# The first 33 score units of an attention and mixture-of-experts block take queries and keys as projected

## The chip, the cores and the metric

The kernel runs on one core of a Trainium2 chip. The metric is the time of one execution on the device in microseconds, the median of several runs. The core's engines are called PE (matrix products), DVE (vector), ACT (scalar functions), POOL (general purpose) and SP (here it only issues DMAs). They run their own instruction streams and meet at semaphores.

## What is computed

Four batch elements of 512 tokens with 256 features go through one transformer block. The first half, with 16 heads of 16 features, is:

```python
h = _layernorm(x, axis=-1) * (1 + ca) + sa
qkv = jnp.einsum('bsh,oh->bso', x, Wqkv) + bqkv
scores = jnp.einsum('bhqd,bhkd->bhqk', q, k) * scale
scores = jnp.where(causal, -jnp.inf, scores)
attn = jax.nn.softmax(scores, axis=-1)
out = jnp.einsum('bhqk,bhkd->bhqd', attn, v)
x = x + ga * _L0_attn_ref(h, ...)
```

The second half normalises again, sends each token to the best of 8 experts, adds a shared expert, and adds the gated sum to x. The gates and shifts (`sa, ca, ga, sb, cb, gb`) come from a small product with `wmod`.

## The kernel before

Products keep float32 accuracy by halves: an operand is split into a float16 high part and a float16 remainder ("low"), and one product is made as high·high, high·low and low·high.

The attention of a batch element b is a loop of 44 steps (`BU`), n = 0 to 43, in each engine's stream. A step holds one **score unit** N of up to 512 columns. The scores are computed twice. The first time, `scores(N)` on PE gives queries on the partitions, and `maxima(N)` on DVE takes each query's maximum. The second time, `scores_t(N)` gives keys on the partitions with the negated maximum built in, and ACT exponentiates the result (`exps`, line 846). The first kind runs ahead of the second by `LAG` = 33 units. So there is a head, b = -1, whose steps n = 11 to 43 hold units 0 to 32 of element 0 and nothing of the second kind. Eleven units make a group of four heads: one of 4 × 128 columns, two of 2 × 256, four of 384 and four of 512.

The units read **stacks**: `qs` and `ks` hold for each head 126 rows with high, high, low of the queries against high, low, high of the keys, so that one product of 126 rows makes all three. Stacks are built through memory. PE projects (`project_qk`, four parts u of an element: queries and keys, each in two halves f), ACT adds the bias and writes high parts and float32 (`qk_parts`, line 835), POOL subtracts for the low parts (`qk_low`, line 700). Then SP stores six pieces to `qk_d` (`qk_out`, line 462) and, when they have landed, loads four back (`stacks`, line 479). Maxima take the same way: DVE negates them (`negate`, lines 1074 and 1075), SP stores them (`maxima_out`, line 489) and loads them into the stacks (line 496).

Meanwhile the experts' weights are split in the background in 27 pieces k. SP loads piece k into `stage` (`stage_load`, lines 512 and 514), ACT makes the high half (`split_high`, line 896), DVE the low half (`split_low`, line 1167), and SP stores both to `w_d` (`halves_out`, line 518). The table `SPLITS` says after which step each split stands: pieces 0 and 1 in the head at steps 18 and 26, pieces 2, 3 and 4 at steps 4, 9 and 14 of element 0. There are two buffers for halves, so the high half of piece 2 waits until `halves_out(0)` has landed, and that of piece 4 until `halves_out(2)` has:

```python
if 2 <= k < BOUNCED:
    ac.wait_ge(s_bw[k % 2], 16 * (k // 2))
```

Other work (projections of the next elements, normalisation, output) stands at steps by the table `SIDE`. These jobs share a bank on PE (`M1`): each waits until the job before it has left it. SP's stream is written out by hand, and every DMA on it waits for the one ahead to be issued. Small rows `mod_d` (line 547) carry the gates through memory.

## Time and profile before

| | us |
|---|---|
| median of 3 runs | 474.42 |
| lowest and highest run | 473.86, 476.61 |
| profiled execution, whole | 479.8 |
| its span | 478.1 |
| PE busy in it | 402.4 |
| DVE busy in it | 310.0 |
| ACT busy in it | 226.8 |

The profiled execution is one of its own; its rows give durations and places in microseconds from the start of the span. "Idle before" is how long the engine had waited, and the arrow names what ended the wait. The head lasts until about 69 us; the rest of element 0 follows until about 124 us.

### The profile page before, as it was taken

How to read it: one execution, taken by the hardware profiler on the slowest of the kernel's cores; microseconds unless marked ns; L12 is line 12 of the kernel's file. 1: busy time of each engine (PE TensorE's matmuls, PEld its weight loads, DVE VectorE, ACT ScalarE, POOL GpSimd, SP SyncE). 2: the span in 40 equal slices, each digit the busy share in tenths (PEclk: the TensorE clock that was granted, in tenths of full speed). 3: DMA queues.
4: the chain of work that ended last, by engine and by line, in shares of the span. 5: the costliest groups of instructions: out<-in, count | busy, mean ns of one | idle time of the engine just before them, and what ended most of it. 6: DMA issues, size and time to landing. Idle time of an engine off the chain costs nothing.

```text
span 478.1 us, 8357 instructions
## 1 busy us (share of the span) xinstructions
PE 402.4 (84%) x2898; PEld 227.9 (48%) x2898; DVE 310.0 (65%) x629; ACT 226.8 (47%) x403; POOL 209.0 (44%) x251
## 2 busy tenths in 40 slices
PE   3767677889978789988879968999968999999991
PEld 3233233444544345444434434565645666666661
DVE  3823697876898968999977753789734444444441
ACT  2533424867666666755677636345122232323220
POOL 1457393374226763358331762110600555555332
PEclk9997789999999999998999989999989999999998
DMA  8568548765678557652433001994621344434210
GB/s 258 170 154 212 147 117 259 265 196 136 168 264 293 156 127 167 222 179 88 169 81 99 2 0 52 354 360 161 180 86 44 65 80 85 78 74 81 32 21 0
DMA packets 45921, 67.95 MB, mean 142 GB/s; under 512 B 5365, under 2 KB 33653, under 8 KB 45881
## 3 DMA queue, kind: packets, MB, share of 16 engines
q1 hardware_dynamic: 40200, 58.76, 40.6%
q0 software_dynamic: 5152, 8.14, 8.6%
q8 instruction: 25, 0.41, 0.4%
q10 hardware_dynamic: 528, 0.52, 0.3%
q14 instruction: 16, 0.12, 0.1%
HBM read 43.14 MB, written 25.18 MB: 143 GB/s over the span
## 4 chain that ended last, share of the span: by engine, by line
PE 51%; DVE 17%; DMA 8%; POOL 7%; issue 7%; ACT 6%; SPq 3%; ACTq 0%; DVEq 0%; POOLq 0%
PE bank L1411 35%; DVE mx L1066 5%; PE bank L1525 4%; PE bank L1509 3%; DVE rowg L1167 2%; PE bank L1739 2%; PE bank L1481 2%; DMA qk_d<-W 2%; POOL W L719 2%; DMA w_d<-rowg 2%; DMA mod_d<-h2T 1%; ACT rowg L896 1%; DMA stage<-in_gup 1%; POOL rowg L727 1%; POOL rowg L726 1%
## 5 line engine op out<-in xcount | busy, mean ns | idle before, releaser
L846 ACT ACTIVATE W<-bank 128x512 f32<-128x512 f32 (+1 forms) x176 | 94.8, 564 | 65.1 <-PE bank L1509 63.3
L1066 DVE TENSOR_REDUCE mx<-bank 128x1 f32<-128x384 f32 (+3 forms) x176 | 104.8, 632 | 20.2 <-PE bank L1483 19.9
L1411 PE MATMUL bank<-W 128*128 128x256 f16 (+2 forms) x756 | 106.5, 293 | 10.2 <-POOL W L694 3.4
L1411 PEld LDWEIGHTS bank<-W 128*128 128x128 f16 x756 | 73.3, 100 | 44.3 <-issue 14.2
L1481 PE MATMUL bank<-W 126*128 126x128 f16 (+3 forms) x256 | 67.0, 318 | 20.6 <-DVE mx L1066 17.2
L719 POOL TENSOR_SCALAR_AFFINE_SELECT W<-W 128x512 f32<-128x512 f32 x64 | 45.3, 713 | 79.7 <-ACT W L846 79.7
L1411 PE MATMUL bank<-W,h2T 128*128 x276 | 68.4, 385 | 4.9 <-DVE W L1182 4.0
L1509 PE MATMUL bank<-W 128*128 128x512 f16 (+3 forms) x256 | 63.1, 304 | 5.2 <-ACT W L846 3.5
L789 POOL DMA_INDIRECT out<-h2T,sidx x23 | 36.3, 1578 | 69.5 <-DVE h2T L1381 69.2
L1525 PE MATMUL bank<-W 128*32 128x128 f32 (+3 forms) x512 | 48.4, 451 | 8.7 <-POOL W L719 8.7
L1483 PE MATMUL bank<-maskb,identb 128*128 128x128 bf16 (+2 forms) x176 | 45.3, 257 | 0.0
L1411 PE MATMUL bank<-h2T,W 128*128 128x512 f16 x192 | 43.1, 379 | 0.6 <-DVE W L1182 0.6
L1481 PEld LDWEIGHTS bank<-W 126*128 126x128 f16 x256 | 24.0, 102 | 40.3 <-DVE mx L1066 28.7
L1411 PEld LDWEIGHTS bank<-W,h2T 128*128 128x128 f16 x276 | 27.1, 98 | 30.8 <-issue 10.6
L1509 PEld LDWEIGHTS bank<-W 128*128 128x128 f16 x256 | 21.5, 98 | 40.3 <-ACT W L846 18.5
L1374 DVE TENSOR_TENSOR W<-bank,W 128x512 f16<-128x512 f32 x23 | 15.9, 692 | 37.4 <-ACT W L979 37.4
L979 ACT ACTIVATE W<-bank 128x512 f16<-128x512 f32 x23 | 13.8, 598 | 55.0 <-PE bank L1739 47.9
L775 POOL DMA_INDIRECT rowg<-h_d,gidx x23 | 23.2, 1009 | 31.4 <-DVE gidx L1324 24.7
L1167 DVE SCALAR_TENSOR_TENSOR rowg<-stage,rowg 128x1024 f16<-128x1024 f32 x18 | 25.2, 1398 | 17.7 <-ACT rowg L896 17.7
L835 ACT ACTIVATE W<-bank,bqk 128x512 f16<-128x512 f32 (+1 forms) x32 | 20.3, 687 | 24.2 <-PE bank L1411 24.2
L1411 PEld LDWEIGHTS bank<-h2T,W 128*128 128x128 f16 x192 | 18.5, 98 | 21.9 <-DVE W L1182 1.0
L700 POOL TENSOR_TENSOR W<-W 128x512 f16<-128x512 f32 x16 | 18.5, 1157 | 17.0 <-ACT W L835 16.7
(163 smaller groups left out, 522.7 us busy)
## 6 DMA issues: line engine op xcount, KB each, us to landing
w_d<-rowg SPq DMA_DIRECT2D x18, 512.0 KB, 3.9
W<-w_d SPq DMA_DIRECT2D x18, 512.0 KB, 8.0
stage<-in_gup SPq DMA_DIRECT2D x16, 512.0 KB
qk_d<-W SPq DMA_DIRECT2D x48, 128.0 KB
W<-qk_d SPq DMA_DIRECT2D x32, 192.0 KB, 4.4
stage<-in_down SPq DMA_DIRECT2D x8, 512.0 KB
x_sb<-in_x SPq DMA_DIRECT2D x4, 512.0 KB, 8.9
h_d<-gbb SPq DMA_DIRECT2D x4, 512.0 KB, 4.5
```

Of the source, the lines that this page charges most:

```text
L719: g.affine_select(out=d, in_=d, compare_op=ALU.is_ge, fill=0.0, base=0, pattern=[[0, 4], [1, P]], channel_multiplier=-1).then_inc(s_msk, 1)
L775: g.indirect_dma_start(rowg[:, r % RG, :], None, h2_d, bass.IndirectOffsetOnAxis(ap=gidx[:, r:r + 1].bitcast(U32), axis=0)).then_inc(s_gr[ ...
L789: g.indirect_dma_start(out.rearrange("b s n -> (b s) n"), bass.IndirectOffsetOnAxis(ap=sidx[:, r:r + 1].bitcast(U32), axis=0), ry[r % YR], ...
L835: a.activation(dst, side_bank("qk", b, u)[:, :], ACT.Identity, bias=bqk[:, 2 * isk + u // 2:2 * isk + u // 2 + 1], scale=1.0 / WS if isk e ...
L846: a.activation(PT[j][:, i:i + m, :], t_bank(N)[:, 0:m * w].rearrange("p (i n) -> p i n", i=m), ACT.Exp).then_inc(s_exp, 1)
L1066: v.tensor_reduce(mx_v[:, b % 2, hp0 // 4, par, i:i + m, t], SB[N % 3][:, 0:m * w].rearrange("p (i n) -> p i n", i=m), AX.X, ALU.max).then ...
L1167: v.scalar_tensor_tensor(split_part(k, 1), staged(k), WS, split_part(k, 0), ALU.mult, ALU.subtract).then_inc(s_el, 1)
L1411: i = t_.matmul(outp, l, r, start=(n == 0), stop=(n == len(prods) - 1), **kw)
L1481: t_.matmul(bk[:, w * i:w * (i + 1)], qs[r][0:P - 2, hp, par, P * t:w], ks[r][0:P - 2, hp, 0:w], start=(i == 0), stop=False, skip_group_ch ...
L1483: t_.matmul(bk[:, 0:m * w].rearrange("p (i n) -> p i n", i=m)[:, :, w - P:w], identb[:, :], maskb[:, :].unsqueeze(1).to_broadcast([P, m, P ...
L1509: q = t_.matmul(t_bank(N)[:, w * i:w * (i + 1)], ks[r][:, hp, P * j:P * (j + 1)], qs[r][:, hp, par, P * j:S], start=True, stop=True)
L1525: q = t_.matmul(OTb[32 * i:32 * i + 32, P * j:S], v1[b % 2][:, c:c + 32], PT[j][:, i], start=(j == 0), stop=(j == TT - 1), tile_position=( ...
```

## The change

Units 0 to 32 no longer read the stacks. `scores_apart` reads the projected queries and keys (`qk0`, now apart from the `qk16` of the other elements) where they lie: 32 partitions hold two neighbouring heads of 16 rows. A copy `qz` of the queries has the other head's rows multiplied by zero (`query_parity` on DVE, eight operations, with a column from `parity_columns`). Each head then takes three products of 32 rows where one of 126 rows stood, and a mask of its own. Neighbouring units go in pairs on two banks and on different 32 rows of the array. Units with several heads run head after head, with a wait (`s_tile`) between them. The head's units rotate over four banks.

The head's table is new (`HEAD`): the jobs for element 1 stand later, the projections at steps 26, 28, 31 and 33, and the splits 0 and 1 at steps 24 and 36. SP's stream is changed in one place. The stacks are still built, for `scores_t` and for the units from 33 on.

```diff
-SPLITS = {-1: {18: 0, 26: 1},
+SPLITS = {-1: {24: 0, 36: 1},
+HEAD = [(12, "stats1", 1, 0), (16, "v", 0, 0), (17, "norm1", 1, 0), (18, "v", 0, 1), (20, "turn", 1, 0),
+        (22, "turn", 1, 1), (26, "qk", 1, 0), (28, "qk", 1, 1), (31, "qk", 1, 2), (33, "qk", 1, 3),
+        (34, "max", 0, 0)]
...
             qk_out(1, 0)
+            maxima_out(0, 0)
+            maxima(0, 0)
             stacks(1, 0)
             qk_out(1, 1)
-            maxima_out(0, 0)
-            maxima(0, 0)
             stacks(1, 1)
...
+            def scores_apart(pair):
...
+                for i in range(m):
+                    c = slice(w * i, w * (i + 1))
+                    if i:
+                        pe.wait_ge(s_tile, n_tile[0])
+                    for N in pair:
+                        t_.matmul(s_bank(N)[:, w * (i + 1) - P:w * (i + 1)], identb[:, :], maskb[:, :],
+                                  start=(i == 0), stop=False, skip_group_check=True)
+                    for p, (cq, ck) in enumerate(((0, 0), (0, 1), (1, 0))):
+                        for N in pair:
+                            j = 32 * (QU[N % UNITS][1] + i)
+                            q = t_.matmul(s_bank(N)[:, c], qz[j:j + 32, cq, f, par, P * t:w],
+                                          qk0[j:j + 32, 2 + ck, f, 0:w], start=False,
+                                          stop=(p == 2 and i == m - 1), skip_group_check=True)
...
+            def query_parity(f, c):
+
+                ve.wait_ge(*((s_ql, 2 * f + 1) if c else (s_qh, 2 * f + 1)))
+                for par in range(2):
+                    v.tensor_scalar(qz[:, c, f, par], qk0[:, c, f], pick[:, par:par + 1], None,
+                                    ALU.mult).then_inc(s_qz, 1)
```

**SP, behind the three loads of `stage` in the head.** `W<-qk_d` are stacks, `ng_d` the maxima, `w_d<-rowg` a store of halves. Before:

```order
L479 DMA W<-qk_d 48x4x512 [waits s_zero,s_const,s_qkw1_0]
L479 DMA W<-qk_d 48x4x512 x3
L462 DMA qk_d<-W 8x16x512 [waits s_qh]
L462 DMA qk_d<-W 8x16x512 x3
L462 DMA qk_d<-W 8x16x512 [waits s_ql]
L462 DMA qk_d<-W 8x16x512
L489 DMA ng_d<-negm 32x2x128 [waits s_neg]
L496 DMA W<-ng_d 2x4x512 [waits s_ngw]
L496 DMA W<-ng_d 2x4x512
L479 DMA W<-qk_d 48x4x512 [waits s_qkw1_1]
L479 DMA W<-qk_d 48x4x512 x3
L518 DMA w_d<-rowg 128x2048 [waits s_el]
```

And after:

```order
L515 DMA ng_d<-negm 32x2x128 [waits s_neg]
L522 DMA W<-ng_d 2x4x512 [waits s_ngw]
L522 DMA W<-ng_d 2x4x512
L505 DMA W<-qk_d 48x4x512 [waits s_zero,s_const,s_qkw1_0]
L505 DMA W<-qk_d 48x4x512 x3
L488 DMA qk_d<-W 8x16x512 [waits s_qh]
L488 DMA qk_d<-W 8x16x512 x3
L488 DMA qk_d<-W 8x16x512 [waits s_ql]
L488 DMA qk_d<-W 8x16x512
L505 DMA W<-qk_d 48x4x512 [waits s_qkw1_1]
L505 DMA W<-qk_d 48x4x512 x3
L544 DMA w_d<-rowg 128x2048 [waits s_el]
```

The store and load of the maxima now stand ahead of the first stacks and of the second set of six stores of element 1, where they stood behind both.

**ACT, between the second job `turn` of element 1 and its projections.** Lines 835 and 861 are `qk_parts`, lines 896 and 922 the split of piece 0. Before:

```order
L835 ACTIVATE W<-bank7,bqk 128x512 [waits s_h1l,s_qkw0_0,s_qkv]
L835 ACTIVATE W<-bank7,bqk 128x512
L896 ACTIVATE rowg<-stage 128x1024 [waits s_eld0]
L835 ACTIVATE W<-bank7,bqk 128x512 [waits s_h1l,s_qkv]
L835 ACTIVATE W<-bank7,bqk 128x512
```

And after:

```order
L922 ACTIVATE rowg<-stage 128x1024 [waits s_eld0]
L861 ACTIVATE W<-bank7,bqk 128x512 [waits s_h1l,s_qkv]
L861 ACTIVATE W<-bank7,bqk 128x512
L861 ACTIVATE W<-bank7,bqk 128x512 [waits s_h1l,s_qkv]
L861 ACTIVATE W<-bank7,bqk 128x512
```

The first of the four parts of element 1 stood ahead of the split; now all four stand behind it.

**PE, in front of the transposition of the maxima** (lines 1489 and 1571). Lines 1481 and 1563 are products of 126 rows, 1483 and 1536 masks, 1541 products of 32 rows, 1411 and 1463 projections. Before, the last units ahead of it are of 512, 4 × 128 and 2 × 256 columns:

```order
L1481 MATMUL bank<-W 128x512
L1483 MATMUL bank<-maskb,identb 128x128
L1481 MATMUL bank<-W 128x128 x4
L1483 MATMUL bank<-maskb,identb 128x512
L1481 MATMUL bank<-W 128x256 x2
L1483 MATMUL bank<-maskb,identb 128x2x128
L1489 MATMUL bank<-ident,mx 32x128
```

And after:

```order
L1463 MATMUL bank<-W 128x512 x6
L1536 MATMUL bank<-maskb,identb 128x128 x2
L1541 MATMUL bank<-W 128x256 x6
L1536 MATMUL bank<-maskb,identb 128x128 x2
L1541 MATMUL bank<-W 128x256 x6
L1571 MATMUL bank<-ident,mx 32x128
```

The fourth projection of element 1, which stood eight steps earlier, now stands right ahead of units 23 and 24 (12 products of 256 columns), and these ahead of the transposition.

## Rows read from the trace of the kernel before

**Rows 1.** The timeline of SP: start, duration, line, what is issued, how many.

```profile
28.41 1.81 SPq L479 DMA_DIRECT2D W<-qk_d  x4
30.27 3.68 SPq L462 DMA_DIRECT2D qk_d<-W  x6
38.61 1.77 SPq L479 DMA_DIRECT2D W<-qk_d  x4
40.43 0.94 SPq L512 DMA_DIRECT2D stage<-in_gup  x2
...
48.54 3.65 SPq L462 DMA_DIRECT2D qk_d<-W  x6
55.07 1.79 SPq L479 DMA_DIRECT2D W<-qk_d  x4
...
65.71 0.31 SPq L489 DMA_DIRECT2D ng_d<-negm  x1
...
67.70 1.76 SPq L479 DMA_DIRECT2D W<-qk_d  x4
69.50 0.44 SPq L518 DMA_DIRECT2D w_d<-rowg  x1
```

**Rows 2.** The timeline of ACT: start, duration, instruction, idle before it and its end.

```profile
46.88 1.06 ACT L896 ACTIVATE rowg<-stage 128x1024 f16<-128x1024 f32 x1 [3.88 <-DMA stage<-in_gup]
47.84 1.25 ACT L835 ACTIVATE W<-bank,bqk 128x512 f16<-128x512 f32 x2
...
69.55 2.77 ACT L846 ACTIVATE W<-bank 128x512 f32<-128x512 f32 x5 [9.08 <-PE bank L1509]
75.64 1.06 ACT L896 ACTIVATE rowg<-stage 128x1024 f16<-128x1024 f32 x1 [3.32 <-DMA w_d<-rowg]
...
87.64 1.06 ACT L896 ACTIVATE rowg<-stage 128x1024 f16<-128x1024 f32 x1 [1.01 <-DMA w_d<-rowg]
```

**Rows 3.** The timeline of DVE and PE where ACT stands at piece 2.

```profile
76.73 1.23 DVE L1167 SCALAR_TENSOR_TENSOR rowg<-stage,rowg 128x1024 f16<-128x1024 f32 x1 [2.46 <-ACT rowg L896]
...
77.14 0.34 PE L1509 MATMUL bank<-W 128*128 128x384 f16 x1 [1.32 <-ACT W L846]
```

**Rows 4.** The chain that ended last, two of its longest pieces behind the head.

```profile
72.24 7.14 DMA mod_d<-h2T
80.25 7.31 DMA w_d<-rowg
```

**Rows 5.** The timeline of PE in the head.

```profile
16.41 7.10 PE L1411 MATMUL bank<-W 128*128 128x512 f16 x24 [3.35 <-POOL W L694]
...
26.97 1.48 PE L1411 MATMUL bank<-W 128*128 128x256 f16 x12
...
35.16 0.61 PE L1481 MATMUL bank<-W 126*128 126x128 f16 x4 [2.84 <-DMA W<-qk_d]
...
43.05 1.47 PE L1411 MATMUL bank<-W 128*128 128x512 f16 x6 [0.81 <-ACT W L835]
...
51.32 2.77 PE L1411 MATMUL bank<-W 128*128 128x512 f16 x6
```

**Rows 6.** Busy time by stretch: PE, PEld, DVE, ACT, POOL, then clock, DMA, GB/s.

```profile
49.80:53.80 4.00, 3.95 (x14) 1.91 (x15) 3.10 (x6) 0.00 (x0) 0.52 (x1) 0.50 0.52 167
```

**Rows 7.** Groups by shape, 16 to 79 us: count, busy, mean ns, idle before.

```profile
L1066 DVE TENSOR_REDUCE mx<-bank 128x1 f32<-128x512 f32 x10 | 6.3, 678 | 1.1 <-PE bank L1483 1.1
L1066 DVE TENSOR_REDUCE mx<-bank 128x1 f32<-128x384 f32 x12 | 6.0, 544 | 1.5 <-PE bank L1483 1.5
...
L1053 DVE SCALAR_TENSOR_TENSOR W<-h2T,W 128x512 f16<-128x512 f32 x1 | 0.7, 681 | 0.0
...
L1483 PE MATMUL bank<-maskb,identb 128*128 128x128 bf16 x30 | 7.3, 242 | 0.0
```

**Rows 8.** The timeline of DVE and PE: negation, and products on single groups of columns.

```profile
65.10 0.27 DVE L1074 TENSOR_SCALAR negm<-bank 32x128 f16<-32x128 f32 x1
...
65.41 0.28 DVE L1075 SCALAR_TENSOR_TENSOR negm<-bank,negm 32x128 f16<-32x128 f32 x1
...
23.44 3.60 PE L1427 MATMUL bank<-stage,cs 128*4 128x512 f32 x8
...
78.86 1.06 PE L1525 MATMUL bank<-W 128*32 128x512 f32 x8
```

More of the change, by code:

```diff
@@ L96 @@
 FIRST = [(2, 4, 7), (7, 10, 13), (13, 15, 18)]
+HEAD = [(12, "stats1", 1, 0), (16, "v", 0, 0), (17, "norm1", 1, 0), (18, "v", 0, 1), (20, "turn", 1, 0),
+        (22, "turn", 1, 1), (26, "qk", 1, 0), (28, "qk", 1, 1), (31, "qk", 1, 2), (33, "qk", 1, 3),
+        (34, "max", 0, 0)]
 def side_jobs(b, n):
-    early = 6 if b < 0 else 0
-    jobs = [(job, b + d, part) for at, job, d, part in SIDE
-            if at - (min(early, at - 2) if d == 2 else 0) == n and 0 <= b + d < B]
+    if b < 0:
+        return [(job, c, part) for at, job, c, part in HEAD if at == n]
+    jobs = [(job, b + d, part) for at, job, d, part in SIDE if at == n and 0 <= b + d < B]
     if b == B - 1:
@@ L235, in build @@
         aT = early(2 * KC * S, F16).rearrange("p (s k n) -> p s k n", s=2, k=KC)
+        at[0] = first
+        qk0 = early(4 * 2 * S, F16).rearrange("p (a c n) -> p a c n", a=4, c=2)
+        qz = early(4 * 2 * S, F16).rearrange("p (c f two n) -> p c f two n", c=2, f=2, two=2)
         bc = early(2 * 3 * H).rearrange("p (r n) -> p r n", r=2)
@@ L262, in build, with s_bank, before, qk_halves @@
         SB = [S0, S1, T2]
+        def s_bank(N):
+            return [S0, S1, T2, OTb][N % 4] if N < LAG else [T2, S0, S1][N % 3]
+        def before(N):
+            return max((n + 1 for n in range(max(N - 4, 0), N) if s_bank(n) is s_bank(N)), default=0)
+        def qk_halves(b):
+            return qk16 if b else qk0
         def t_bank(N):
@@ L927, in _ @@
                         exps(BU * b + n)
+                    if b < 0 and n == 15:
+                        modulation_rows()
+                        other_high()
                     if n % UNITS == 4 and G > 0:
@@ L1460, in project_v @@
                 i.then_inc(s_qkv, 1)
+            n_tile = [0]
+            def scores_apart(pair):
+                gr = pair[0] // UNITS
+                par, f = gr % 2, gr // 2
+                t, _, m = QU[pair[0] % UNITS]
+                w = P * (t + 1)
+                if pair[0] == 0:
+                    pe.wait_ge(s_const, 2)
+                    pe.wait_ge(s_col, 1)
+                if pair[0] % (2 * UNITS) == 0:
+                    pe.wait_ge(s_qz, 4 * f + 4)
+                    pe.wait_ge(s_ql, 2 * f + 2)
+                if max(before(N) for N in pair):
+                    pe.wait_ge(s_mx, max(before(N) for N in pair))
+                for i in range(m):
[11 more added lines that the diff above has]
+                                          stop=(p == 2 and i == m - 1), skip_group_check=True)
+                            if p == 2 and i == m - 1:
+                                q.then_inc(s_s1, 1)
+                    if i < m - 1:
+                        n_tile[0] += 1
+                        q.then_inc(s_tile, 1)
             def scores(N):
@@ L1500, in scores_t @@
                     pe.wait_ge(s_mr, 2)
-                before = [n for n in range(max(N - 3, 0), N) if t_bank(n) is t_bank(N)]
-                if before:
-                    pe.wait_ge(s_exp, before[-1] + 1)
+                    pe.wait_ge(s_stk[0][0], 16 * 4)
+                used = [n for n in range(max(N - 3, 0), N) if t_bank(n) is t_bank(N)]
+                if used:
+                    pe.wait_ge(s_exp, used[-1] + 1)
                 if t_bank(N) is T2:
@@ L1517, in values @@
                     pe.wait_ge(s_v, TT * (b + 1))
-                if j == 0 and G:
-                    pe.wait_ge(s_ote, G)
+                if j == 0:
+                    pe.wait_ge(*((s_ote, G) if G else (s_mx, LAG)))
                 pe.wait_ge(s_msk, 4 * G + j + 1)
```

94 lines of the change are left out of this document (58 added, 36 removed).

## The prediction

> **What bounds the kernel now.** I read the waits first. In the head, PE stands until the stacks have landed: the first unit starts at 35.16 us, after 2.84 us of waiting, while the projections ended at 23.51 [rows 5]. The change is aimed at these 11.65 us. But the head's end is not what ACT waits for last. ACT exponentiates the first five units from 69.55 us, and then waits 3.32 us, until 75.64, for the store of halves [rows 2]. DVE stands at the same piece 2 (2.46 us of waiting) and PE behind ACT's banks (1.32 us) [rows 3]. So at 75.64 us all three engines stand at one point. It depends on one DMA, the store that SP issued at 69.50 [rows 1]. Two long pieces of the chain that ended last, 72.24 to 79.38 and 80.25 to 87.56, are the DMAs that SP issued next [rows 4], and ACT waits once more, 1.01 us, until 87.64 [rows 2]. **The question is therefore when SP issues the store of halves 0 (line 518), not when the first unit starts.** Until it has landed, whatever the head gains is waited away.
>
> **SP before.** Negated maxima leave at 65.71, the last stacks at 67.70, the store at 69.50: 3.79 us from negation to store [rows 1].
>
> **SP after.** Behind the negation stand: store and load of the maxima; the stacks (1,0); the six stores of part f = 1 of element 1; their landing; the stacks (1,1); then the store of halves.
> - Store and load of the maxima: 65.71 to 67.70, 1.99 us [rows 1].
> - The rest: the rows have the very sequence once, for element 0: stacks at 28.41, six stores from 30.27, stacks at 38.61, next issue at 40.43. That is 12.02 us. The lower bound takes the landing from the third set, which nothing was in front of: 48.54 to 55.07 is 6.53 us, with stacks of 1.81 ahead and 1.79 behind, 10.13 us [rows 1]. I take 12.02, since here too four stacks go out right ahead of the stores.
> So negation to store is 14.0 us (12.1 to 14.0) against 3.79. To come out even, the negation would have to end 10.2 us earlier than at 65.7, at 55.5.
>
> **When the negation ends after.** Its start is anchored by a load that the change leaves alone: SP's stream up to the loads of `stage` at 40.43 us is the same, so piece 0 lands at 46.88 as before, ACT makes its half and reaches `qk_parts` at 47.84 [rows 1, 2]. Before, this was the second part of element 1. After, it is the first, since all four now stand behind the split. It ends at 49.1. Three projections are left, each behind ACT's reading of the one before it. On PE the following stand in a row, in the new order:
> - projection, part 1: six products of 512 columns, 1.47 us [rows 5]
> - units 18, 19 and units 20, 21: a pair is six products of 512 columns in all, as a projection is, so 1.47 us if they run one after the other and about 0.75 if they run two by two, with 0.1 for masks: 3.1 or 1.7 us for both pairs [rows 5]
> - projection, part 2: 1.47 us
> - unit 22, four heads one after the other, in each a mask and three products of 128 columns; one takes 0.242 us from start to end, and 0.06 more for each that follows in the stream [rows 5, 7]: about 1.7 us
> - projection, part 3: 1.47 us
> - units 23, 24: 12 products of 256 columns, 1.48 us, or half, with masks and one wait between heads 0.4: 1.9 or 1.1 us [rows 5]
> - transposition and negation: from the rows 0.27 and 0.28 us with what lies between, about 1.0 [rows 8]
> ACT's 1.25 us for each part [rows 2] is covered by the pairs, but for 0.2 us once where they run side by side. The sums are 12.1 and 10.1 us, so the negation ends at 61.2 or 59.2 us. The rows show PE's clock at 0.50 from 49.8 to 53.8, after it had stood idle, and a projection at 51.32 taking 2.77 us in place of 1.47 [rows 5, 6]. PE will again wait for ACT before 49 us. A clock at half for one projection adds 1.3 us, for the pair behind it up to 1.5: 63 us at most. I take **60.5 us**, between 59.2 and 63.
>
> DVE does not bound this: from 49.2 us on it has 10 maxima of 0.54 to 0.68 us [rows 7], 6.4 us, against PE's 10 or more.
>
> **What goes before 49 us at no cost.** DVE's eight operations on the queries are not in the trace. The bounds are 0.27 us (negation, 128 columns) and 0.68 (a remainder of 512 columns) [rows 7, 8], so 2.2 to 5.4 us; I take 2.4. PE's first unit starts about 24 us. Fourteen units must be through by 47.9, when DVE will stand at the split, and side jobs of some 7 us lie between; at 0.68 a unit DVE needs 17 of the 22 us. The slack is 3 to 5 us, and it covers the longer operations, the extra products (three of 32 rows for each of 126) and the gates' products, 3.60 us [rows 8]. Without that cover each microsecond would be paid once.
>
> **Two rules of the Trainium skill.** The trace has matmuls side by side only on groups of columns: eight records of 512 columns take 1.06 us, where eight on one place took 3.60 [rows 8]. Of groups of rows no row tells. "TensorE: Matmul & The Clock Gate", in its part on packing small matmuls, says that products on different row groups run together; by it the negation would end at 59.2 and the time would be about 478.1. "TensorEngine Tiling (Array Packing)", Key Properties, says that a change of the tiling mode drains the engine. Masks here take the whole array and the products 32 rows, so each step would be drained twice; by that rule the 61.2 would be nearer. Neither gives another sign.
>
> **The sum.** 60.5 + 14.0 = 74.5 us for the issue of the store, against 69.50: 5.0 us later. Bounds: 59.2 + 12.1 = 71.3, so 1.8 us later; 63 + 14.0 = 77.0, so 7.5 later. As ACT, DVE and PE all wait at that point, and the DMAs next on SP (4) stand behind the same store, nothing absorbs it: ACT waited 3.32 us and will wait longer, since its exponentials start earlier, at about 65.5 us (five maxima and the split of piece 1, 1.23 us, lie between the negation and the bank of the last unit). Behind this point the order of all streams is as before, so the rest moves as a whole. The profiled execution was 479.8 us (span 478.1), 5.4 over the median of 474.42; the shift applies to either. 479.8 becomes 484.8, and the median **479.4 us**.
>
> **Rivals.**
> 1. *The order on SP costs almost nothing.* Products side by side, PE's clock at full and the stores landed as fast as in the third set: 1.8 us later, 476.2; with DVE or ACT a little sooner 1 us, 475.4. For it: PE stays busy longer before 49 us. Against it: two independent favourable cases. Chance 0.18.
> 2. *The head's gain arrives: faster.* The place is ACT's wait at piece 2. If the store of halves were issued ahead of where it was, the gain would be the earlier start of the second kind of units, 69.1 to about 65: 4 us, 470.4. It decides at a negation that ends at 55.5 us. It needs three projections and their reading, 3 × (1.47 + 1.25) from 49.1, to be over at 54.5 already without this rival's units; they are over at 57.3. It is possible only if piece 0 lands well ahead of 46.88. Chance 0.07.
> 3. *The small products are the bound.* At half clock a 512-column product takes 0.43 us (the first of the 24 at 16.41 ran so). If the 32-row products leave PE's clock there, and run one after the other, a unit of 1,583 columns on average takes 1.3 us and some waits, about 1.7 instead of 0.9; over the 16 units until the second projection that is 13 us, less 3 of slack: 10 us more, 489 (and up to 9 more if the low clock stays to the negation). For it: a group of eleven units has 17,408 columns where it had 7,168. Against: PE is busier than before, and idleness went ahead of the low clock in [rows 5, 6]. Chance 0.09.
> 4. *The change does not do what it says*, the units still wait for something near 35 us: then unit 13 is reached at about 52, and the shift is 3 us more than forecast, 482. It is inside my case, not counted apart.
>
> **How the numbers follow.** The forecast case, 2.4 to 9 us later, has 0.66. Left out of the range are rival 2 (0.07), rival 3 (0.09) and little else, so the range goes from 474.9 to 485.5. About 0.5% is what a measurement of this kernel can tell from no change, 2.4 us. Faster by more: rival 2, 0.07. Within: rival 1, 0.18, with some of it beyond, 0.17. Slower by more: 0.76.
>
> **What would show it.** Right: the first unit of 32 rows at about 24 us; ACT's first split still at 46.9; negation at 59 to 63; the store of halves issued at 72 to 77; ACT's wait for `w_d` at piece 2 grown from 3.3 us to about 12, and the split there at about 80.6. Overlap of pairs shows in two products of one pair starting together. Wrong: a negation before 56, a store of halves before 70, or an ACT that is not waiting for it at piece 2. If piece 0 lands several microseconds earlier or later, the anchor is wrong and all moves with it.

## The result and the profile after

The changed kernel took 481.17 us in the median (480.63 to 483.48), the kernel before beside it 475.38 us (473.86 to 476.61): a ratio of 1.0113, with a 95% interval of 1.0076 to 1.0150. It is slower, by 5.8 us. The ratios and intervals in this document are taken over the fast runs alone and need not equal the quotient of the medians, which cover all runs (the two differ by up to 0.3%). The profiled execution took 481.26 us, with a span of 479.5 us and a clock of 0.956.

| | before | after |
|---|---|---|
| first unit on PE | 35.16 us | 23.80 us |
| ACT's split of piece 0 | 46.88 | 47.34 |
| negation ends | 65.69 | 61.10 |
| store of halves 0 issued | 69.50 | 75.53 |
| ACT's split of piece 2 | 75.64 | 81.51 |
| ACT's split of piece 4 | 87.64 | 93.31 |

The timeline of SP after, the answer to [rows 1]: start, duration, line, what is issued, how many.

```profile
61.12 0.34 SPq L515 DMA_DIRECT2D ng_d<-negm  x1
62.60 0.56 SPq L522 DMA_DIRECT2D W<-ng_d  x2
63.27 1.76 SPq L505 DMA_DIRECT2D W<-qk_d  x4
65.08 3.66 SPq L488 DMA_DIRECT2D qk_d<-W  x6
73.71 1.77 SPq L505 DMA_DIRECT2D W<-qk_d  x4
75.53 0.44 SPq L544 DMA_DIRECT2D w_d<-rowg  x1
```

The maxima leave at 61.12, 4.6 us earlier than the 65.71 of [rows 1]. The store of halves leaves at 75.53, 6.0 us later than the 69.50 there. Between them lie 14.41 us in place of 3.79. SP issues nothing from 68.74 (the end of the six stores) to 73.71: it waits until the stores have landed. The chain that ended last has this landing as a piece, and the two pieces of [rows 4] again behind it:

```profile
68.16 5.54 DMA qk_d<-W
...
78.23 6.88 DMA mod_d<-h2T
...
85.98 7.24 DMA w_d<-rowg
```

The timeline of ACT, the answer to [rows 2]. The last columns are the idle time before an instruction and what ended it.

```profile
47.34 1.06 ACT L922 ACTIVATE rowg<-stage 128x1024 f16<-128x1024 f32 x1 [3.03 <-DMA stage<-in_gup]
48.44 1.26 ACT L861 ACTIVATE W<-bank,bqk 128x512 f16<-128x512 f32 x2
...
58.58 1.26 ACT L861 ACTIVATE W<-bank,bqk 128x512 f16<-128x512 f32 x2 [2.14 <-PE bank L1463]
...
67.14 0.60 ACT L872 ACTIVATE W<-bank 128x512 f32<-128x512 f32 x1 [5.05 <-PE bank L1592]
...
81.51 1.06 ACT L922 ACTIVATE rowg<-stage 128x1024 f16<-128x1024 f32 x1 [9.72 <-DMA w_d<-rowg]
```

The first exponential starts 2.4 us earlier than in [rows 2], and the wait for the store of halves has grown from 3.32 to 9.72 us. DVE and PE stand at the same place, as in [rows 3]. The timeline of DVE, then that of PE:

```profile
19.41 0.61 DVE L1261 TENSOR_SCALAR W<-W,pick 128x512 f16<-128x512 f16 x2 [1.92 <-ACT W L861]
...
22.09 6.11 DVE L1261 TENSOR_SCALAR W<-W,pick 128x512 f16<-128x512 f16 x6
...
60.82 0.28 DVE L1106 SCALAR_TENSOR_TENSOR negm<-bank,negm 32x128 f16<-32x128 f32 x1
...
82.60 1.23 DVE L1198 SCALAR_TENSOR_TENSOR rowg<-stage,rowg 128x1024 f16<-128x1024 f32 x1 [8.76 <-ACT rowg L922]
```

```profile
45.68 2.72 PE L1463 MATMUL bank<-W 128*128 128x512 f16 x6 [0.25 <-POOL W L719]
...
49.76 2.15 PE L1463 MATMUL bank<-W 128*128 128x512 f16 x6
51.74 0.28 PE L1536 MATMUL bank<-maskb,identb 128*128 128x128 bf16 x2
51.95 0.82 PE L1541 MATMUL bank<-W 32*128 32x512 f16 x6
52.70 0.28 PE L1536 MATMUL bank<-maskb,identb 128*128 128x128 bf16 x2
...
53.67 1.47 PE L1463 MATMUL bank<-W 128*128 128x512 f16 x6
54.98 0.22 PE L1536 MATMUL bank<-maskb,identb 128*128 128x128 bf16 x1
55.13 0.34 PE L1541 MATMUL bank<-W 32*128 32x128 f16 x3
55.53 0.23 PE L1536 MATMUL bank<-maskb,identb 128*128 128x128 bf16 x1
...
65.10 1.46 PE L1541 MATMUL bank<-W 32*128 32x512 f16 x6
...
83.00 0.50 PE L1592 MATMUL bank<-W 128*128 128x384 f16 x1 [7.62 <-ACT W L872]
```

From 81.51 us on everything is shifted as a whole: the split of piece 4 by 5.67 us, of piece 6 (106.28 against 100.50) by 5.78, and of the last piece, 26 (278.87 against 273.12), by 5.75. The medians differ by 5.79.

The two profiled spans, 478.1 and 479.5 us, differ by less. The busy time by stretch shows why. Its columns are those of [rows 6]. First before, then after:

```profile
330.00:350.00 20.00, 16.71 (x115) 10.02 (x113) 14.48 (x36) 4.70 (x9) 8.33 (x8) 1.00 0.51 159
350.00:370.00 20.00, 17.00 (x107) 11.11 (x108) 8.07 (x17) 4.41 (x9) 0.00 (x0) 0.91 0.08 27
```

```profile
330.00:350.00 20.00, 19.32 (x158) 12.08 (x156) 17.93 (x51) 7.62 (x13) 5.14 (x6) 1.00 0.47 157
350.00:370.00 20.00, 17.31 (x114) 11.01 (x112) 9.74 (x20) 4.79 (x9) 3.67 (x3) 1.00 0.35 110
```

The execution of before that was profiled has 2.6 us more idle PE time in the first stretch and a clock of 0.91 in the second. The first scatter of results on POOL behind them is shifted by only 2.06 us (372.18 and 374.24). So the profiled execution of before lost 3.7 us in between which the other did not. This stretch, from the split of piece 26 to the first scatter, takes 94.7 to 100.4 us over the profiled executions, and not by their head: 99.06 in before, 95.37 in the changed kernel, but 99.4 and 100.4 in e3 and e1, which are changed kernels too. The execution of before was also 5.4 us above its own median. The shift up to piece 26 is therefore the better measure of the change, and the medians agree with it.

### The profile page after: what moved, and what is told of

The parts are those of the page before. It is cut to its first block, busy times and chain, and to the rows that moved or that the text cites. A ratio compares the mean times of both kernels' runs of the same rounds, so it can differ in the third digit from the quotient of the medians.

```text
span 479.5 us, 8593 instructions
## 1 busy us (share of the span) xinstructions
PE 414.1 (86%) x3009; PEld 230.8 (48%) x3009; DVE 317.1 (66%) x639; ACT 226.7 (47%) x403; POOL 210.3 (44%) x251
## 4 chain that ended last, share of the span: by engine, by line
PE 55%; DVE 17%; POOL 7%; issue 6%; ACT 6%; DMA 5%; SPq 2%; ACTq 0%; DVEq 0%; POOLq 0%
PE bank L1463 35%; PE bank L1608 4%; DVE mx L1097 4%; PE bank L1592 3%; PE bank L1829 2%; DVE rowg L1198 2%; PE bank L1563 2%; PE bank L1541 2%; POOL W L745 2%; ACT W L847 2%; DMA w_d<-rowg 2%; DMA mod_d<-h2T 1%; POOL rowg L753 1%; POOL rowg L752 1%; DMA qk_d<-W 1%
## 5 line engine op out<-in xcount | busy, mean ns | idle before, releaser
L1097 DVE TENSOR_REDUCE mx<-bank 128x1 f32<-128x384 f32 (+3 forms) x176 | 105.7, 633 | 19.1 <-PE bank L1565 11.3
L1463 PE MATMUL bank<-W 128*128 128x256 f16 (+2 forms) x756 | 107.9, 295 | 8.2 <-POOL W L719 3.6
L1592 PE MATMUL bank<-W 128*128 128x512 f16 (+3 forms) x256 | 65.1, 312 | 11.5 <-ACT W L872 9.8
L1463 PE MATMUL bank<-W,h2T 128*128 x276 | 67.2, 380 | 1.8 <-DVE W L1213 1.0
L1563 PE MATMUL bank<-W 126*128 126x128 f16 (+3 forms) x208 | 54.7, 314 | 6.5 <-DVE mx L1097 6.5
L1565 PE MATMUL bank<-maskb,identb 128*128 128x128 bf16 (+2 forms) x143 | 36.2, 253 | 0.0
L1563 PEld LDWEIGHTS bank<-W 126*128 126x128 f16 x208 | 19.5, 100 | 18.3 <-DVE mx L1097 11.7
L726 POOL TENSOR_TENSOR W<-W 128x512 f16<-128x512 f32 x16 | 19.7, 1233 | 16.1 <-ACT W L861 15.9
```

The lines of the kernel that those rows point to most:

```text
L1097: v.tensor_reduce(mx_v[:, b % 2, hp0 // 4, par, i:i + m, t], s_bank(N)[:, 0:m * w].rearrange("p (i n) -> p i n", i=m), AX.X, ALU.max).then ...
L1463: i = t_.matmul(outp, l, r, start=(n == 0), stop=(n == len(prods) - 1), **kw)
L1563: t_.matmul(bk[:, w * i:w * (i + 1)], qs[r][0:P - 2, hp, par, P * t:w], ks[r][0:P - 2, hp, 0:w], start=(i == 0), stop=False, skip_group_ch ...
L1565: t_.matmul(bk[:, 0:m * w].rearrange("p (i n) -> p i n", i=m)[:, :, w - P:w], identb[:, :], maskb[:, :].unsqueeze(1).to_broadcast([P, m, P ...
L1592: q = t_.matmul(t_bank(N)[:, w * i:w * (i + 1)], ks[r][:, hp, P * j:P * (j + 1)], qs[r][:, hp, par, P * j:S], start=True, stop=True)
```

## The experiments

There are two theories. **A**: the store of halves stands behind stores, a landing and stacks on SP, and that order alone costs the time. **B**: the new head (products of 32 rows, later projections) costs it. A landmark serves for all runs: the start of ACT's split of piece k, in us.

| kernel | k = 2 | 4 | 6 | 7 | 26 | ratio to before |
|---|---|---|---|---|---|---|
| before | 75.64 | 87.64 | 100.50 | 124.19 | 273.12 | 1 |
| changed | 81.51 | 93.31 | 106.28 | 129.95 | 278.87 | 1.0113 |
| a0_changed_again | 81.06 | 92.80 | 105.83 | 129.50 | 278.51 | 1.0132 |
| e1_sp_order | 79.58 | 91.34 | 104.57 | 128.25 | 278.70 | 1.0077 |
| e2_before_sp | 87.01 | 98.62 | 111.78 | 135.47 | 284.43 | 1.0236 |
| e3_stores_first | 72.15 | 92.92 | 106.22 | 129.89 | 278.86 | 1.0108 |
| e4_split_late | 82.08 | 93.85 | 106.70 | 130.37 | 279.24 | 1.0140 |
| e6_unit_by_unit | 82.39 | 94.17 | 107.16 | 130.84 | 279.81 | 1.0168 |
| e5_stores_free | 74.05 | 85.65 | 105.97 | 129.11 | 279.55 | 1.0082 |
| e7_before_free | 72.65 | 84.40 | 105.49 | 128.63 | 279.08 | 1.0095 |
| e8_maxima_first | 72.33 | 83.94 | 97.85 | 125.12 | 274.02 | 0.9985 |
| e9_before_maxima | 73.91 | 85.68 | 99.61 | 125.06 | 274.10 | 1.0005 |
| e10_maxima_again | 71.69 | 83.29 | 97.22 | 120.91 | 269.85 | 0.9951 |
| e11_before_again | 73.07 | 84.84 | 98.77 | 122.44 | 271.31 | 0.9955 |

Runs that shared a chip share the runs of the kernel before: e1 to e4 (480.45 us there), e5 to e7 with the changed kernel again (475.65), e8 and e9 (475.64), e10 and e11 (475.86). Only ratios are compared across these groups. The landmarks come from one profiled execution each. They scatter: two executions of the changed kernel (changed and a0) differ by 0.4 to 0.5 us, and e6, whose edit changes nothing that its rows show, lies another 0.9 us behind changed.

### The order on SP, undone and done alone

e1_sp_order is the changed kernel with SP's order of before:

```diff
             qk_out(1, 0)
-            maxima_out(0, 0)
-            maxima(0, 0)
             stacks(1, 0)
             qk_out(1, 1)
+            maxima_out(0, 0)
+            maxima(0, 0)
             stacks(1, 1)
```

> The changed kernel with SP's stream in the head as before: stacks (1,0) and the six stores of part f = 1 ahead of the maxima. Theory A (SP's order sets when the store of halves 0 goes out, and ACT, DVE and PE wait for it at piece 2): the stores of f = 1 go out near 61 us, their low parts at about 65 (POOL makes them behind the gates' rows), the maxima at about 65.5 in place of 61.1, the store of halves at about 71.3 in place of 75.53, ACT's split of piece 2 at about 77.4 in place of 81.51. Time 4.1 us less than the changed kernel, about 477, still 1 to 2 us above the kernel before. Theory B (the small products in the head cost the time, the order on SP none): no change against the changed kernel, 481.

e2_before_sp is the kernel before with the opposite edit, the order of the changed kernel.

> The kernel before with one edit, SP's new order in the head (maxima ahead of stacks (1,0) and of the stores of f = 1). Nothing of the small products is in it. Theory A: negation ends at 65.7 as before, the store of halves goes out 14 us later at about 79.7 in place of 69.50, ACT's split of piece 2 is at about 85.8, and the time is 10 us more than before, 485.5. Theory B: no change, 475.4.

Measured: e2 491.10 us, ratio 1.0236 (1.0206 to 1.0266). That is 10.65 us more than before by the medians, as theory A had it. In its timeline of ACT the wait at piece 2 has become:

```profile
87.01 1.06 ACT L896 ACTIVATE rowg<-stage 128x1024 f16<-128x1024 f32 x1 [13.38 <-DMA w_d<-rowg]
```

So moving two calls, one store and two loads on SP, cost nearly 11 us without anything else of the change. In e2 the store of halves was issued at 81.19, 14.2 us behind the issue of the maxima (67.01). It left 11.7 us later than before: 10.4 are this distance (3.79 before), and 1.3 are a later negation, which the edit does not touch. The rest of the change takes 5 to 6 us of it back (1.0236 against 1.0113), as its negation ends 5.9 us earlier than that of e2 (61.10 against 66.98).

e1 took 484.12 us, ratio 1.0077 (1.0052 to 1.0102). By the ratios this is only some 2 us better than the changed kernel (1.0113 and 1.0132 in its two measurements), not the 4.1 expected, and the intervals overlap, so the time alone does not show a gain. Piece 6 is 1.7 us earlier. Its timeline of SP shows why:

```profile
62.29 4.58 SPq L488 DMA_DIRECT2D qk_d<-W  x6
66.91 0.47 SPq L515 DMA_DIRECT2D ng_d<-negm  x1
71.31 0.54 SPq L522 DMA_DIRECT2D W<-ng_d  x2
```

The maxima now leave behind the six stores, at 66.91, and their small store takes 4.4 us until the load goes out; ahead of the stores it took 1.48 (61.12 to 62.60). So the first exponential comes at 73.82, the store of halves at 73.69, and ACT's wait at piece 2 is 1.11 us. Neither order lets the earlier negation through: in the one the store of halves waits, in the other the maxima do. Besides, e1 lost another 1.6 us between pieces 11 (151.79, against 147.74 before) and 12 (164.63 against 159.01), as e5 and e7 did. There PE's granted clock was lower (see the section on the prediction).

### The store of halves first

e3_stores_first is the changed kernel with halves 0 and 1 ahead of the small stores and the stacks of element 1:

```diff
+            halves_out(0)
+            stage_load(3)
             qk_out(1, 0)
             maxima_out(0, 0)
             maxima(0, 0)
+            halves_out(1)
+            stage_load(4)
             stacks(1, 0)
             qk_out(1, 1)
             stacks(1, 1)
-            for k in range(2):
-                halves_out(k)
-                stage_load(k + 3)
```

> The changed kernel, with the store of halves 0 and the load of piece 3 ahead of the stores of element 1 on SP, and those of halves 1 and piece 4 right behind the maxima. The work is the same. Theory A: ACT no longer waits at piece 2 and splits it at about 72 us, as soon as its first five exponentials are done, in place of 81.51 (75.64 before). If nothing else is late behind it, the time is 3.8 us below the kernel before, 471.6; the gates' rows, which go out behind the stacks (1,1) at about 77, or the store of halves 2 may take back 1 to 3 us. Range 470.5 to 475. Theory B: 481, as the changed kernel.

Measured: 485.23 us, ratio 1.0108 (1.0070 to 1.0147), no gain at all: theory A's 470.5 to 475 us, below the kernel before, was missed. The wait at piece 2 is gone: the split starts at 72.15 us, 9.4 earlier. The timeline of ACT has it at piece 4 now:

```profile
92.92 1.06 ACT L923 ACTIVATE rowg<-stage 128x1024 f16<-128x1024 f32 x1 [9.06 <-DMA w_d<-rowg]
```

Halves 2 were issued at 85.45, behind the landing of the same six small stores (77.92) and that of `mod_d` (79.73 to 84.59). My expectation had followed the path only up to the wait it removed.

### The anchor

e4_split_late holds back the split of piece 0 on ACT:

```diff
-SPLITS = {-1: {24: 0, 36: 1},
+SPLITS = {-1: {34: 0, 36: 1},
```

> The changed kernel with the split of piece 0 at step 34 in place of 24, behind all four projections of element 1. It tests the anchor of the prediction, that ACT reaches the parts of element 1 only when piece 0 has landed. In the trace of the changed kernel ACT was through with the split at 48.40 us and PE with the first projection at 48.40 as well, at the low clock. If the landing alone is the anchor, the parts start up to 3 us earlier, the negation ends at about 58.5 in place of 61.1 and the time is 478.5. If PE's projection is as late, which I think, nothing moves but by 1 us: 480 to 481.5.

Measured: 486.29 us, ratio 1.0140 (1.0103 to 1.0176). With ACT free of the load, the first part of element 1 was still read only at 49.91 us, behind a projection at half clock:

```profile
49.91 1.26 ACT L861 ACTIVATE W<-bank,bqk 128x512 f16<-128x512 f32 x2 [4.71 <-PE bank L1463]
```

```profile
47.23 2.64 PE L1463 MATMUL bank<-W 128*128 128x512 f16 x6
```

So the landing of piece 0, on which I had anchored the sum, is one of two things that end together. The other is PE with this projection. In the changed kernel it starts at 45.68 and takes 2.72 us, so it ends at 48.40, just where ACT's split ends. Without the landing, ACT could have gone on no earlier there either. The run itself is less clean: in it the projection stood 1.55 us later, because PE was at half clock from about 42.7 us on (in the changed kernel from about 44.3), and the edit does not touch that. It shows that ACT then waited for PE and not for the landing; it does not show what an earlier projection would have brought.

### The products of a pair, one unit after the other

e6_unit_by_unit issues the three products of a pair's first unit ahead of those of the second, where the change alternates:

```diff
-                    for p, (cq, ck) in enumerate(((0, 0), (0, 1), (1, 0))):
-                        for N in pair:
+                    for N in pair:
+                        for p, (cq, ck) in enumerate(((0, 0), (0, 1), (1, 0))):
```

> The changed kernel with the three products of a pair's first unit ahead of the three of the second, where they alternated. The rows of the changed kernel have six products of 512 columns in 0.82 us from first start to last end, where six of a projection take 1.47. If only neighbours in the stream on different groups of rows run together, a pair of 512 columns now takes about 1.3 us (only one of the three overlaps), the chain to the negation is 1.5 us longer and the time 1.5 us more. If the engine looks further than the next product, nothing changes.

The timeline of PE of e6:

```profile
52.97 0.83 PE L1541 MATMUL bank<-W 32*128 32x512 f16 x6
53.72 0.29 PE L1536 MATMUL bank<-maskb,identb 128*128 128x128 bf16 x2
```

Six products from start to next start take 0.75 us, exactly as with alternation (51.95 to 52.70), where six on the whole array take 1.31. In both kernels two of the six have started within 0.05 us of the first, the sign of overlap that the prediction named. The time was 483.66 us, ratio 1.0168 (1.0119 to 1.0217), against 482.06 us and 1.0132 (1.0099 to 1.0166) for the changed kernel measured again beside it; the intervals overlap, and the profiled spans were 479.7 and 479.0. The order within a pair is not what makes the products run side by side, and it is not where the time went. For the changed kernel measured again stood:

> The changed kernel as it is, beside the three that follow and the kernel before on one chip, so that their differences can be taken from it. Expected 1.2% over the kernel before (1.0113 in its first comparison), with the store of halves 0 issued near 76 us and ACT's split of piece 2 near 82.

### SP laid out anew, in three steps

If theory A holds, a layout of SP exists in which the head's gain arrives. e5_stores_free sets one up for the changed kernel: the small stores of (1,1) and their stacks go far back, and halves 0 to 3 stand between the rest. Here (b, f) means element b, half f.

```diff
+            halves_out(0)
+            stage_load(3)
             qk_out(1, 0)
             maxima_out(0, 0)
             maxima(0, 0)
             stacks(1, 0)
-            qk_out(1, 1)
-            stacks(1, 1)
-            for k in range(2):
-                halves_out(k)
-                stage_load(k + 3)
+            halves_out(1)
+            stage_load(4)
             sp.wait_ge(s_m4, 1)
             sp.dma_start(mod_d[:, :], m4[:, :]).then_inc(s_md, 16)
+            halves_out(2)
+            stage_load(5)
...
+            qk_out(1, 1)
+            halves_out(3)
+            stage_load(6)
+            stacks(1, 1)
...
```

e7_before_free has the same layout in the kernel before.

> The changed kernel with SP's stream in the head laid out so that no store of halves stands behind a long landing: halves 0 and the load of piece 3 ahead of the stores of element 1; behind the maxima stacks (1,0), halves 1, the gates' rows out, halves 2, and only then the gates' rows back in, the stores of f = 1 of element 1, halves 3 and the stacks (1,1). In the run with only halves 0 and 1 moved, the wait had gone from piece 2 to piece 4 (9.06 us, until 92.92), because halves 2 still stood behind the stacks (1,1). Theory A: with this the waits at pieces 2 and 4 are both gone, ACT splits piece 2 at about 73 and piece 4 at about 84.5 in place of 93.31, and the time falls by 8 to 9 us against the changed kernel and by 2 to 4 us against the kernel before (ratio 0.992 to 0.996). Theory C (another wait of the same length always takes the place, since memory traffic is the bound): 1.008 or more.

> The kernel before with the same layout of SP's stream. Its waits for stores of halves were 3.32 us at piece 2 and 1.01 us at piece 4. Theory A: both go, 3 to 4 us less than before (ratio 0.991 to 0.994). What the 32-row products are worth by themselves is the difference to the run above: the first exponential was at 67.14 us with them and at 69.55 without, but the fifth ended at 71.8 and 72.3, so between 0.5 and 2.4 us. If the ratio is 1.00 here, the store was not the bound of the kernel before either, and my reading of its wait at piece 2 was wrong.

Measured: e5 480.92 us, ratio 1.0082 (1.0051 to 1.0113); e7 481.20 us, 1.0095 (1.0060 to 1.0131). Both miss theory A. The 1.0082 of e5 even lies where theory C, that another wait always takes the place, had put it (1.008 or more). e7 was to be faster than before and is slower by 5.5 us by the medians, 4.5 by its ratio. Pieces 2 to 5 are early in both (piece 4 at 85.65 and 84.40 against 87.64), and then the gain goes at one point. The timeline of ACT of e7:

```profile
99.18 0.60 ACT L851 ACTIVATE W<-bank 128x512 f32<-128x512 f32 x1 [5.46 <-PE bank L1514]
```

and that of SP:

```profile
89.15 1.79 SPq L479 DMA_DIRECT2D W<-qk_d  x4
91.00 0.43 SPq L489 DMA_DIRECT2D ng_d<-negm  x1
96.39 0.53 SPq L496 DMA_DIRECT2D W<-ng_d  x2
```

The maxima of the second half of element 0 had come to stand behind the stacks of (1,1): issued at 91.00, loaded at 96.39, where the kernel before has 88.70 and 91.53. The load is 4.9 us later, and so is the split of piece 6 (5.0).

e8_maxima_first (from the changed kernel) and e9_before_maxima (from the kernel before) move these maxima and two more stores of halves ahead of the small stores and the stacks of (1,1). The code is shown against e5 and e7; in the loop behind it these jobs are left out for element 0:

```diff
-            qk_out(1, 1)
             halves_out(3)
             stage_load(6)
+            maxima_out(0, 1)
+            maxima(0, 1)
+            halves_out(4)
+            stage_load(7)
+            qk_out(1, 1)
+            halves_out(5)
+            stage_load(8)
             stacks(1, 1)
...
```

> Changed kernel with the layout of SP's instructions of e5_stores_free, in which one thing more is moved: the store and the load of the maxima of (0,1) stand ahead of the small stores and the stacks of (1,1), and the halves of pieces 4 and 5 stand ahead of those stores and stacks too. The split of piece 5 was at 92.92 us in e5_stores_free, at 93.85 before; there ACT then waited for PE and PE for the maxima of (0,1), and the split of piece 6 came at 105.97. Theory A (what ACT and PE wait for is whatever stands behind a landing on SP; a layout can clear all of them): the maxima's load is issued near 91 us, piece 6 is split near 99.5 us (100.50 before), and the whole is 474 to 476 us, ratio 0.990 to 1.000. Theory B (what is freed at one place is lost at the next, since the small stores and stacks of (1,1) have to go somewhere before the second half of element 1): 478 to 482 us, with a wait of several us at a store of halves or at the products of element 1 later on.

> Kernel before with the same layout of SP's instructions as e8_maxima_first. In e7_before_free the split of piece 4 was at 84.40 us (87.64 before) and the gain was lost at 99.18 in a wait of 5.46 us for the maxima of (0,1). Theory A: that wait goes, piece 6 is split near 98 us against 100.50, and the whole is 472 to 474 us, ratio 0.992 to 0.998. Theory B: a new wait takes it, 475 to 481 us. If both theories hold in part, e9 is under e8 by the 1.2 us or so by which its first stores of halves are earlier.

Measured: e8 476.02 us, ratio 0.9985 (0.9953 to 1.0017); e9 476.75 us, 1.0005 (0.9977 to 1.0033). The whole loss of the change is gone, but neither is faster than before. e8 lies in theory A's range (0.990 to 1.000); e9 misses it (0.992 to 0.998). Piece 6 was early as expected (97.85 and 99.61 against 100.50), piece 7 late (125.12 against 124.19). The timeline of SP of e8:

```profile
112.27 1.79 SPq L505 DMA_DIRECT2D W<-qk_d  x4
114.10 0.44 SPq L515 DMA_DIRECT2D ng_d<-negm  x1
119.22 0.53 SPq L522 DMA_DIRECT2D W<-ng_d  x2
```

and of ACT:

```profile
121.60 0.60 ACT L884 ACTIVATE W<-bank 128x512 f32<-128x512 f32 x1 [3.24 <-PE bank L1604]
```

Once more maxima stand behind stacks, those of (1,0) behind the stacks of (2,0). The negation had ended at 112.28.

e10_maxima_again and e11_before_again exchange these two as well (shown against e8 and e9):

```diff
                     qk_out(b + 2, 0)
-                    stacks(b + 2, 0)
+                    if b:
+                        stacks(b + 2, 0)
                 if b + 1 < B:
                     maxima_out(b + 1, 0)
                     maxima(b + 1, 0)
+                if b == 0:
+                    stacks(2, 0)
```

> Kernel of e8_maxima_first with one more pair moved: in the pass of element 0 the maxima's store and load of (1,0) stand ahead of the stacks of (2,0). In e8_maxima_first the negation of (1,0) ended at 112.28 us, its store was issued at 114.10 behind the stacks (which waited for the landing of the small stores of (2,0)), its load at 119.22, and ACT waited 3.24 us for PE until 121.60; the split of piece 6 (97.85) was 2.65 us earlier than before, that of piece 7 (125.12) 0.9 us later. Theory A (this was the next thing behind a landing): the store is issued at 112.3, the load by 114.5 to 116, the split of piece 7 comes at 120 to 122.5 us, and the whole at 472.5 to 474.5 us, ratio 0.991 to 0.997. Theory B (the landing itself is slow because the stores, loads and stacks share the 16 DMA engines at 400 GB/s there): the load is issued at 117 or later and the whole stays at 475 to 477 us.

> Kernel before with the same layout as e10_maxima_again. In e9_before_maxima the split of piece 6 was at 99.61 us, the maxima's load of (1,0) at 120.30. Theory A: load by 116 to 118, piece 7 at 122 to 124 us, the whole 1.5 to 1.8 us above e10_maxima_again, since its first stores of halves and so all its pieces up to 6 are that much later (99.61 against 97.85): 474 to 476 us. Theory B: equal to e10_maxima_again within 0.5 us, as e8 and e9 were. So the difference of the two is what the change itself gives or takes when nothing behind a landing is in its way.

Measured: e10 472.64 us, ratio 0.9951 (0.9924 to 0.9977); e11 473.79 us, 0.9955 (0.9934 to 0.9977). The timeline of SP of e10:

```profile
111.69 0.33 SPq L515 DMA_DIRECT2D ng_d<-negm  x1
113.11 0.55 SPq L522 DMA_DIRECT2D W<-ng_d  x2
113.77 1.76 SPq L505 DMA_DIRECT2D W<-qk_d  x4
```

The same store takes 1.42 us ahead of the stacks and took 5.12 behind them, so the slow landing was not due to traffic that would be there in any order. e10 came out as theory A said (store at 111.69, load at 113.11, piece 7 at 120.91, 472.64 us), and theories B and C are excluded by it. e11 was to be 1.5 to 1.8 us above e10 and is 1.15 above it. Piece 7 is split at 120.91, 3.3 us earlier than before, and this stays: 3.27 at piece 26, 3.2 in the medians, 2.3 by the ratio. **Both are faster than the kernel before, by about half a per cent, and e10 is 1.6% faster than the changed kernel by their ratios** (0.9951 and 1.0113), with the same work.

What the change itself gives, once the waits found here are out of its way, is the difference of e10 and e11: 1.55 us at piece 6, 1.46 at piece 26, 1.15 in the medians, but only 0.2 by the ratios. By time the two can't be told apart (the intervals of their ratios overlap), and the landmarks of one execution scatter by nearly as much. So that the 32-row products gain anything is not shown.

## Why the prediction was right

479.4 us were forecast, 4.98 more than before; the medians differ by 5.79. Step by step:

- **What bounds**: that all hangs on the issue of the store of halves held. e2, with SP's order alone, lost 10.65 us, and its shift passed through undiminished from piece 2 (11.4 us) to piece 26 (11.3).
- **From negation to store**: 14.0 us forecast, 14.41 measured. Store and load of the maxima took 2.15 (forecast 1.99), the rest 12.26 (forecast 12.02, from the same sequence for element 0). Taking the slow landing and not that of the third set was right: the landing took 5.54 us here.
- **The anchor**: 46.88 forecast, 47.34 measured. The number held, the reasoning only in part: the landing is not alone there, as PE's projection at half clock ends at the same moment (48.40). That this number came out right is partly luck, as the split of piece 0 started between 45.78 and 48.58 us over the runs that left it in its place.
- **The negation**: 60.5 forecast, 61.10 measured. Its terms, from start to start in the timeline of PE: projection 1.98 (forecast 1.47; low clock), units 18 to 21 1.93 (forecast 1.7 side by side), projection 1.31, unit 22 2.09 (forecast 1.7), projection 1.31, units 23 and 24 1.52 (forecast 1.9 or 1.1), transposition and negation 1.20 (forecast 1.0), from 49.76 on. The case side by side, which came, had been summed to 59.2; 60.5 was a choice within its bounds. The 1.9 us between 59.2 and 61.10 are the later start (0.7), the first projection at half clock (0.5) and the units (1.0), among small amounts that cancel. The upper bound was added up wrongly: by its own terms, 61.2 with 1.3 and 1.5 for the clock, it is 64.0 and not 63. Unit 22 was under-sized: a head takes 0.55 us and not 0.42. Between two heads lies the wait `s_tile`, and from the start of the three products to the next mask 0.40 us pass.
- **The store of halves**: 74.5 forecast, 75.53 measured; ACT's split 80.6 forecast, 81.51 measured.
- **ACT's wait**: about 12 us forecast, 9.72 measured. The exponentials began at 67.14 and not at 65.5: the last pair in front of them ran at half clock (1.46 us where 0.82 stood), and the first products of the second kind took 0.63 us for 512 columns, where those of before take 0.38. So the five of them took 4.65 us, not 2.77. It cost nothing, as the wait covers it.
- **The head before 49 us**: DVE's eight operations were taken at 2.4 us, in bounds of 2.2 to 5.4. They took 6.7 us, outside the bounds (the last section). The slack of 3 to 5 us held it, and the first unit started at 23.80 (forecast 24). That this error had no price is luck: the slack was not meant for it alone.
- **Rival 1** (475.4 to 476.2) needed PE's clock at full and a fast landing. Neither came. **Rival 3** did not come: pairs ran side by side. Nor did **rival 4**: the units no longer wait for the stacks.
- **Rival 2** put the gain at 4 us, if the store of halves did not stand in the way. That was too simple, and so were my expectations for e3, e5 and e7. With the store gone from the way (e3), the whole gain was waited away at piece 4, with that one cleared (e5) at the maxima of (0,1), then (e8) at those of (1,0). Only e10 is 3.2 us faster than before (2.3 by its ratio), and 2.1 of it come from the layout without the change (e11).

Products side by side was the case that the Trainium skill, "TensorE: Matmul & The Clock Gate", in its part on packing small matmuls, stated for row groups. The trace agrees: six products of 32 × 512 take 0.75 us, where six on the whole array take 1.31. Of the rule in "TensorEngine Tiling (Array Packing)", Key Properties, that a change of mode drains the engine, the rows bound the price. For a pair of one head, mask to mask, 0.96 us pass (51.74 to 52.70). Three times the 0.218 us of a whole-array product, 0.65, is what six take two by two. So masks, both changes of mode and any wait together cost at most 0.31 us.

The profiled e1, e5 and e7 lost 1.6 us between pieces 11 and 12, which the others did not. The traces say where it went: with the same 89 products, PE was busy for 11.3 us of that stretch at a granted clock of 0.89 or 0.90, against 9.73 at 1.00 in all the others, and the stretch took 12.85 us in place of 11.27. Why the clock was lower there stays open. No run isolates it.

## What to carry over

A delay in front of a wait that all engines share is paid in full, but an advance lasts only to the next wait, and on a queue that is issued in order that is the next instruction behind a landing. Before moving anything on such a queue, list what stands behind each landing and when it is ready. Small transfers that others wait for at once (here the maxima) go ahead of transfers that are needed late (here stacks). A change of the layout should also be tried in the kernel before: here all of the gain that is shown was there already (0.9955 without the change, 0.9951 with it).

## What was not expected of the hardware

**A small store behind others.** `ng_d`, 16 KB, from issue to the issue of its load: 1.41 to 1.75 us for the first maxima of element 0 with nothing right ahead of them (before, after, e10), 4.4 behind six small stores (e1), 5.0 to 5.7 behind four stacks (e5, e7, e8, e9). The place on the queue costs 3 to 4 us for a transfer that itself takes 1.4. The second maxima of element 0 took 2.7 to 2.8 us in after and before, but 1.4 to 1.6 in e8 to e11. In all six a store of halves (512 KB) had left 4.2 us earlier, so that store is not the difference; what is stays open. The Trainium skill, "DMA: Bandwidth & Descriptors", Queues, rings and completion order, says that the increment of a semaphore lands only after every earlier write of the same DMA engine. These numbers agree with it, and the pair of e8 and e10 (5.12 and 1.42 us for the same store) is the plainest case.

**The masked queries.** The eight operations of one shape (line 1261, in the timeline of DVE above) took from 229 to 2196 ns. The first two took 0.61 us together, from 19.41 us on, where POOL had been idle until 19.96. The other six took 6.11 us, from 22.09 to 28.20, and beside them POOL worked almost without a gap. The timeline of POOL:

```profile
22.25 3.74 POOL L726 TENSOR_TENSOR W<-W 128x512 f16<-128x512 f32 x3 [1.13 <-ACT W L861]
25.93 1.02 POOL L666 MEMSET W<- 128x1104 f32 x1
27.00 1.04 POOL L668 MEMSET W<- 128x1104 f32 x1
```

Of the six, the first took 0.23 us, before POOL started at 22.25; the other five took 1.2 us each in the mean. So alone such an operation takes 0.23 to 0.35 us, near the lower end of my bounds (0.27), and beside POOL more than the upper end (0.68). No run has moved POOL's work away, so that POOL is the cause is not shown. The Trainium skill, "SBUF — State Buffer", Who interferes with whom, says that VectorE and GpSimd share one pair of ports under an exclusive lock. The durations agree with that: an operation that has to wait for the end of one of POOL's would take up to the latter's 1.0 to 1.3 us, or twice that.

**The clock.** Busy time by stretch, with the columns of [rows 6]:

```profile
24.00:35.00 11.00, 10.75 (x63) 3.50 (x63) 10.56 (x18) 2.23 (x5) 10.43 (x22) 0.84 0.56 140
43.00:49.00 6.00, 5.68 (x34) 2.09 (x32) 2.52 (x5) 2.93 (x4) 1.15 (x1) 0.61 1.07 295
...
49.80:53.80 4.00, 4.00 (x23) 1.47 (x24) 2.71 (x6) 1.26 (x2) 1.65 (x2) 0.83 0.02 4
```

The third row answers [rows 6]: where the clock was 0.50 before, it is 0.83, with PE busy throughout. Yet just ahead of it, from 43 to 49 us, it is 0.61, though PE was busy for 5.68 of the 6 us. I had put the low clock down to idleness alone, and that does not fit this row: the clock was still 1.00 from 43 to 44 us and fell at about 44.3, behind 4.7 us of masks, transpositions and 32-row products in which PE was busy for 4.45. Then it was 0.50 until about 50.5. It had been low once before, in the stretch of the first row: 0.54 from 27.3 to 31.0 us, with PE never idle, behind three units of such products. There the gates' products took 3.54 us for four, where eight took 3.60 before [rows 8]. Both falls came behind small products, as rival 3 had feared, but both times the clock came back. That the small products are the cause is not shown.
